# A fused state-space and feed-forward kernel: two factor blocks are centred by TensorE and ScalarE, and GpSimd makes one more C product in step 5

## The reference

```
xc   = silu(conv4(ctx @ in_proj^T) + conv_b)            # 512 channels x 512 times
dt_low, B, C = split(x_proj @ xc)                       # 16 + 16 + 16 rows
dt   = softplus(dt_proj @ dt_low + dt_proj_b)           # 512 channels x 512 times
state[n] = state[n] * exp(dt * A[n]) + dt * xc * B[n]   # 16 states per channel, a scan over time
y    = sum_n state[n] * C[n] + D * xc
x1   = x + (y * silu(layernorm(x)))^T
out  = x1 + layernorm(x1) @ (sum_r factors[r]) / sqrt(8) + bias
```

## Time and profile before

| | |
|---|---|
| median of 3 runs | 496.18 us (495.03 to 500.95) |
| the profiled execution | 495.23 us, span 493.4 us |
| busy: DVE, POOL, PE, ACT | 466.9 us (95%), 452.2 (92%), 434.0 (88%), 349.4 (71%) |
| chain that ended last, by engine | DVE 36%, issue 23%, POOL 15%, PE 13%, ACT 5%, DMA 5% |
| mean granted clock of TensorE | 0.962 of full speed |

### The profile page before, as it was taken

The page is one execution under the profiler, slowest core; times in us unless marked ns, Lnnn a source line. Parts: engine busy times, 40 slices in busy tenths (PEclk is TensorE's granted clock), DMA queues, the critical chain, the costliest instruction groups (busy, mean ns, idle before and its releaser), DMA issues.

```text
span 493.4 us, 4146 instructions
## 1 busy us (share of the span) xinstructions
PE 434.0 (88%) x1058; PEld 183.5 (37%) x1066; DVE 466.9 (95%) x364; ACT 349.4 (71%) x625; POOL 452.2 (92%) x236
## 2 busy tenths in 40 slices
PE   8769897999798788999988799879888997998797
PEld 5223343434243232434333244424433343443342
DVE  4899999999999999999999999999999979999895
ACT  2789655977589868897778877788699585734422
POOL 4379899999899999999999999999999978999992
PEclk9979998999899989999999999989999699999899
DMA  6799744439981000200891000000593000000002
GB/s 188 249 362 340 193 83 99 84 71 222 321 317 57 0 0 0 64 3 27 307 374 45 1 21 0 21 0 2 181 408 140 1 21 21 22 23 21 0 0 85
DMA packets 17871, 53.96 MB, mean 109 GB/s; under 512 B 2724, under 2 KB 3236, under 8 KB 16824
## 3 DMA queue, kind: packets, MB, share of 16 engines
q1 hardware_dynamic: 16696, 45.31, 25.4%
q0 software_dynamic: 1152, 8.39, 8.5%
HBM read 49.24 MB, written 4.46 MB: 109 GB/s over the span
## 4 chain that ended last, share of the span: by engine, by line
DVE 36%; issue 23%; POOL 15%; PE 13%; DMA 5%; ACT 5%; SPq 2%; DVEq 0%; POOLq 0%; ACTq 0%
DVE dA L980 18%; POOL h L1131 11%; PE y L524 8%; DVE h L980 7%; DVE h L986 4%; DMA b_rep<-bc_scratch 4%; DVE acc L937 3%; POOL h L1124 3%; PE work L501 2%; ACT dA L799 1%; DVE work L957 1%; DVE work L951 1%; SPq L346 1%; PE work L433 1%; POOL fsum L1157 1%
## 5 line engine op out<-in xcount | busy, mean ns | idle before, releaser
L1131 POOL TENSOR_TENSOR h<-b_rep,dtu 128x1024 f32<-128x1024 f32 x127 | 303.3, 2444 | 13.1 <-DMA b_rep<-bc_scratch 11.1
L524 PE MATMUL y<-h,ident 128*128 128x512 f32 x508 | 248.6, 627 | 39.2 <-DVE h L986 37.8
L799 ACT ACTIVATE dA<-dt,a_neg 128x512 f32<-128x512 f32 x256 | 165.8, 679 | 85.9 <-DVE h L986 71.6
L980 DVE TENSOR_TENSOR_SCAN dA<-dA,h 128x1024 f32<-128x1024 f32 x84 | 191.9, 2285 | 1.5 <-ACT dA L799 1.4
L524 PEld LDWEIGHTS y<-h,ident 128*128 128x128 f32 x508 | 95.3, 197 | 177.2 <-issue 109.2
L1124 POOL TENSOR_TENSOR h<-h,c_rep 128x1024 f32<-128x1024 f32 x44 | 104.9, 2384 | 5.2 <-DVE h L980 5.1
L980 DVE TENSOR_TENSOR_SCAN h<-dA,h 128x1024 f32<-128x1024 f32 x44 | 100.3, 2280 | 2.7 <-ACT dA L799 2.7
L986 DVE TENSOR_TENSOR h<-dA,c_rep 128x1024 f32<-128x1024 f32 x83 | 101.1, 1219 | 1.4
L413 PE MATMUL work<-ctx_sb,w_in 128*128 128x512 f32 x60 | 29.2, 614 | 1.6 <-DVE x L1022 1.2
L517 PE MATMUL work<-fsum,xnT 128*128 128x512 f32 x64 | 28.8, 592 | 0.0
L937 DVE SCALAR_TENSOR_TENSOR acc<-work,chan,acc 128x511 f32<-128x511 f32 (+2 forms) x30 | 21.6, 731 | 5.8 <-ACT acc L658 5.7
(11 more groups left out here) (137 smaller groups left out, 422.8 us busy)
## 6 DMA issues: line engine op xcount, KB each, us to landing
b_rep<-bc_scratch SPq DMA_DIRECT2D x32, 512.0 KB, 9.2
c_rep<-bc_scratch SPq DMA_DIRECT2D x32, 512.0 KB, 8.5
fsum<-factors POOLq DMA_DIRECT2D x8, 1024.0 KB, 8.8
x<-x SPq DMA_DIRECT2D x4, 1024.0 KB, 8.2
out<-x SPq DMA_DIRECT2D x16, 256.0 KB, 2.0
ctx_sb<-ctxT SPq DMA_DIRECT2D x3, 512.0 KB, 6.2
ctx_sb<-ctxT SPq DMA_DIRECT2D x2, 256.0 KB, 4.0
w_in<-w_inT SPq DMA_DIRECT2D x1, 384.0 KB, 4.8
```

The lines of the kernel that those rows point to most:

```text
L524: mm = pe.matmul(y[:], ident[:], h[:, (s * PAIRS + j) % H_RING, i, :], start=False, stop=(j == sum_order(s)[-1] and i == 1))
L799: act.activation(dA[:, j % 2, i, :], dt[:, k % 2, :], ACT.Exp, scale=a_neg[:, k, 2 * j + i:2 * j + i + 1]).then_inc(exp_done, 1)
L980: dve.tensor_tensor_scan(pair if on_pool(s * PAIRS + j) else decay, decay, pair, 0.0, ALU.mult, ALU.add).then_inc(scanned, 1)
L1131: pool.tensor_tensor(h[:, (s * PAIRS + j) % H_RING], b_rep[:, j], dtu[:, k % 2, :].unsqueeze(1).to_broadcast([P, 2, L]), ALU.mult).then_in ...
```

## The change

In step 5, PE and ACT centre the blocks 0 and 1 of `fsum`: PE adds block and mean row in `work1` by two identity matmuls (`factor_centre`), after the sums of index 0 and 1, and ACT's scaling reads `work1` instead of `fsum`. For this ACT stores the mean row negated, and POOL's `centre` adds it. ACT's four scalings move from the slots 4, 5, 6, 7 to the slots 1, 2, 6, 7; POOL centres blocks 2 and 3 alone, in the slots 4 and 6. The turn of t = 0 moves from index 0 to index 2, since `work1` is taken before that. In step 5 POOL also makes the C product of pair 5, and PE adds the pairs in the order 1, 0, 3, 2, 4, 6, 5, 7.

```diff
-SCALE_SLOTS = (4, 5, 6, 7)
-CENTRE_SLOTS = (2, 4, 5, 6)
+SCALE_SLOTS = (1, 2, 6, 7)
+CENTRE_SLOTS = (4, 6)
+TENSOR_CENTRE = 2
+MIDDLE_POOL_C = (0, 2, 4, 5)
+MIDDLE_SUM_ORDER = (1, 0, 3, 2, 4, 6, 5, 7)
...
+            early[0] = early[0][:TURN] + ((KB + 1, 2),) + early[0][EVAC:]
...
-            return j in (LAST_POOL_C if s == STEPS - 1 else EARLY_POOL_C if s < KB else POOL_C)
+            return j in (LAST_POOL_C if s == STEPS - 1 else EARLY_POOL_C if s < KB else MIDDLE_POOL_C if s == KB + 1 else POOL_C)
...
-                    sp.wait_ge(f_centred, KB)
+                    sp.wait_ge(f_summed, TENSOR_CENTRE)
+                    sp.wait_ge(f_centred, KB - TENSOR_CENTRE)
...
                 if t > 0:
                     pe.wait_ge(t_final, t)
+                else:
+                    pe.wait_ge(f_scaled, TENSOR_CENTRE)
...
+            def factor_centre(k):
+                pe.wait_ge(f_mean_evac, 1)
+                if k > 0:
+                    pe.wait_ge(f_scaled, k)
+                pe.matmul(work1[:], ident[:], fsum[:, k, :], start=True, stop=False)
+                pe.matmul(work1[:], ident[:], row_b[:], start=False, stop=True).then_inc(f_summed, 1)
...
+                    if s == KB + 1 and i < TENSOR_CENTRE:
+                        factor_centre(i)
...
                     if s == KB + 1 and j in SCALE_SLOTS:
                         i = SCALE_SLOTS.index(j)
-                        act.wait_ge(f_centred, i + 1)
-                        act.activation(fsum[:, i, :], fsum[:, i, :], ACT.Copy, scale=FR ** -0.5).then_inc(f_scaled, 1)
+                        if i < TENSOR_CENTRE:
+                            act.wait_ge(f_summed, i + 1)
+                        else:
+                            act.wait_ge(f_centred, i + 1 - TENSOR_CENTRE)
+                        act.activation(fsum[:, i, :], work1[:] if i < TENSOR_CENTRE else fsum[:, i, :], ACT.Copy, scale=FR ** -0.5).then_inc(f_scaled, 1)
...
-                        act.activation(row_b[:], work1[:], ACT.Copy).then_inc(f_mean_evac, 1)
+                        act.activation(row_b[:], work1[:], ACT.Copy, scale=-1.0).then_inc(f_mean_evac, 1)
...
-                pool.tensor_tensor(fsum[:, k, :], fsum[:, k, :], row_b[:], ALU.subtract).then_inc(f_centred, 1)
+                pool.tensor_tensor(fsum[:, k, :], fsum[:, k, :], row_b[:], ALU.add).then_inc(f_centred, 1)
...
-                        centre(CENTRE_SLOTS.index(j))
+                        centre(TENSOR_CENTRE + CENTRE_SLOTS.index(j))
```

More of the change, by code:

```diff
@@ L200, in build @@
         f_centred = sem("f_centred")
+        f_summed = sem("f_summed")
         row_landed = sem("row_landed")
@@ L256, in on_pool @@
             s, j = divmod(p, PAIRS)
-            return j in (LAST_POOL_C if s == STEPS - 1 else EARLY_POOL_C if s < KB else POOL_C)
+            return j in (LAST_POOL_C if s == STEPS - 1 else EARLY_POOL_C if s < KB else MIDDLE_POOL_C if s == KB + 1 else POOL_C)
         def sum_order(s):
-            return LAST_SUM_ORDER if s == STEPS - 1 else EARLY_SUM_ORDER if s < KB else SUM_ORDER
+            return LAST_SUM_ORDER if s == STEPS - 1 else EARLY_SUM_ORDER if s < KB else MIDDLE_SUM_ORDER if s == KB + 1 else SUM_ORDER
         def tensor_convs(n):
```

## The result

| | before | changed |
|---|---|---|
| median (lowest to highest) | 495.61 us (491.75 to 500.95, 6 runs) | 511.92 us (507.55 to 516.34, 6 runs) |
| profiled execution, span | 495.23 us, 493.4 us | 512.58 us, 510.8 us |
| busy DVE, POOL, PE, ACT | 466.9, 452.2, 434.0, 349.4 us | 466.1, 450.8, 443.3, 349.7 us |

The ratio is 1.0355, with a 95% interval of 1.0308 to 1.0403. 509 was forecast, within 503 to 514.

What follows compares the result with a forecast made beforehand. The prediction took DVE, 95% busy and back to back in step 5, as the bound. Stalls of 10.1 and 3.0 us plus 1.7 for PE's clock, less 1.15, gave +13.7 on 495.23 us: 509 us, range 503 to 514.

Steps and rivals of the forecast that it cites:

- First gap: Step 5, before DVE's scan of pair 2: DVE stands still 10.1 us, as ACT's slot 1 waits for PE's factor_centre(0).
- Second gap: Step 5, before DVE's scan of pair 5: ACT's exponentials wait for the moved turn, 3.0 us, with or without the first stall.
- clock term: PE's path to the second stall in step 5: half clock after idleness costs 1.7 us, bounds nothing and 3.6 us.
- The C product: Pair 5 in step 5 leaves DVE for POOL: 1.15 us won, with POOL's product in time by 3.6 us.
- the lateness is constant: Sign: from step 6 on, the rows are those of before, later by a constant near 13.7 us.
- absorbed: Rival, chance 0.09: both stalls happen, but part comes back in DVE's 11.8 us of later idle time; 501 to 506 us.
- Hidden: Rival, chance 0.06: ACT's wait in slot 1 of step 5 costs nothing, so the kernel is not slower; 494 to 498 us.
- larger: Rival, chance 0.09: PE's clock stays low, its path costs 3.6 us and step 6 runs late too; 511 to 514 us.

Runs made afterwards that it cites:

- e3: The changed kernel with only ACT's scalings of blocks 0 and 1 moved from slots 1 and 2 to 3 and 4; 0.9998 of the kernel before's time.
- e5: The changed kernel with ACT's four softplus operations in slot 1 of step 5 done ahead of the wait for factor_centre(0); 1.0225 of the kernel before's time.
- e6: The changed kernel with useless matmuls added in two idle stretches of PE in step 5; 506.12 us, 1.0239 of the kernel before's time.
- e7: The changed kernel without POOL's C product of pair 5 in step 5, and with the old sum order; 1.0351 of the kernel before's time.
- e1: The kernel before with only the turn of t = 0 moved from index 0 to index 2 of step 5; 1.0077 of the kernel before's time.
- e2: The kernel before with only POOL's C product of pair 5 in step 5 and the new sum order; 1.0025 of the kernel before's time.
- e4: The changed kernel with ACT's scalings in slots 4 to 7, turn copy in slot 6, t = 1 statistics in slot 7; 0.9983 of the kernel before's time.
- e10: The kernel of e4 without POOL's C product of pair 5 in step 5, products and sum order as before; 0.9963 of the kernel before's time.

## Why the prediction was right

**First gap.** Forecast 10.1 us, measured 10.01. The working held link by link: `factor_centre(0)` from 178.22 (178.29 forecast), ACT's scaling at 180.14 and not 180.17, exponentials at 183.19, the scan at 184.50 (184.6). e3 took the wait from its place and the gap went; e5 took the 2.5 us of softplus from behind it and 2.54 went. What the working didn't say is that its start, PE's sum of pair 1 at 176.21, already held 1.6 us of slow clock; with a high clock the gap is 8.42 (e6, e7). That 10.1 and 10.01 agree to 0.1 us is luck in this part: the trace of before and that of the changed kernel met the same low clock there.

**Second gap.** Forecast 3.0 us and 1.7 for the clock, measured 15.66 - 10.01 = 5.65. e6 shows the two apart: 2.94 without the clock, so the clock term was mis-sized, 2.7 us and not 1.7. The granted clock stayed low through the input projection and into the sum of pair 3, within the bounds of 0 and 3.6 which the prediction kept. That the gap doesn't hang on the first one was forecast and is shown by e1. By the Trainium skill ("TensorE: Matmul & The Clock Gate", section "What's actually happening") the clock is throttled by default and activity releases it. The trace agrees: 8.31 us idle, then 0.50.

**The C product.** Forecast -1.15 us, measured 14.40 - 15.66 = -1.26. That it would stay won was wrong. The prediction asked whether POOL's product would be in time for y, counted PE's sum of it before DVE's last product, and found 3.6 us to spare. The product was in time (POOL's ended at 205.3), but in the changed order PE adds pair 5 only behind pair 6, whose product DVE made first at 206.8. So PE had three pairs left to add from 206.88 on, after 3.54 us of idleness:

```profile
206.88:213.83 6.95, 6.95 (x12) 2.98 (x13) 6.95 (x6) 6.04 (x10) 6.16 (x4) 0.75 0.00 0
```

In e6, at the high clock, two sums took 3.70 us, and the last began 1.82 us before the layer. An estimate from these rows has the first two done at 210.6 here, the last product of DVE ready at 210.8 and the layer begun at 212.6, as late as DVE was. At a granted clock of 0.75 on the mean the three took 6.95 us, the layer of t = 0 began at 213.83, 15.57 us late, and step 6 gave back 1.18 us. By e6 and e7 it takes both, the order and the clock: e6 has the same order at the high clock, and lost nothing. e7 has the order of before and met the low clock too (12 records in 7.06 us), but they began at 202.58 and were done 0.88 us before DVE's last product: it lost nothing either. In e2 and e4 the cause is another one, POOL's product itself comes too late.

**The rest.** From step 7 to step 9 the lateness is constant within 0.03 us, as forecast, though at 15.6 us and not at 13.7. Behind it the traces differ, and not by this change alone: the changed kernel goes from 15.6 at step 9 to 19.9 at the end of step 12 and 18.2 at the end, e10 from 0.00 to 1.28, e1 from 4.65 to 0.18. Nine of the eleven traces of the experiments come out of step 13 some 3.4 us earlier against before than they went in, so here it is the trace of before that lost time. In it ACT waits 4.60 us for a turn on PE, in a stretch of low clock (10.24 us from 381.76). I ascribe the differences behind step 9 to the clock; no run isolates it.

**The sum.** 13.7 us forecast; 15.6 by the scans, 16.3 by the medians. The missing 1.9 are 1.0 of the clock in the second gap and 1.2 in step 6, less 0.2 of small terms. The rival "absorbed" failed as argued: POOL came out of step 5 with a lead, waited 0.79 and 2.10 us for scans in step 6, and DVE got nothing of it. "Hidden" failed with the 10.98 us that ACT waited in slot 1. The "larger" rival, which had 0.09, was half right: 511.92 lies in its 511 to 514 as well as in the forecast's 506 to 512, PE's path cost 2.7 us, midway between the 1.7 of the forecast and its 3.6, and step 6 did run late by the clock, as it said. The forecast left that last part out of its sum.

## What to carry to other kernels

A wait put into an engine's list costs what is queued behind it, not what the waiting work takes: write down what the engine must do next and by when, then when the awaited result can be there, and only then look at busy shares. Here ACT was 71% busy and had 1.6 us of slack at the place. Work taken off the bounding engine is won only if the engine that takes it delivers before the next join; ask when the result is ready, how many operations of the joining engine are left from then on in its own order, and what they take at the lower clock. Where the whole time spreads by several microseconds, compare the starts of one repeated instruction instead: where the matmul engine met the same clock in both traces, a difference of 0.1 us can be read from one trace each.

## What the runs showed that was not expected

Matmuls of no use, placed in idle stretches of PE on the way of a late chain, took 2.7 us off one gap and 1.2 us off the next stage (e6), at no cost that the scans show. And the same code ahead of step 5 met the low clock in one trace and not in another, which moved the first gap between 8.42 and 10.01 us in kernels with the same list for ACT; such a term belongs in the range of every forecast in which a chain leads over PE.
